# Two float32r parts instead of three bf16 parts for the first expert layer's up products

## The reference, cut to what matters

```
h      = xn @ Wm + bm                       # 128 features = 8 heads of 16
t      = h.reshape(tokens * 8, 16)
w      = softmax(t @ expert_emb)            # 16 experts, the best two kept
hmid   = gelu(einsum('td,edi->tei', t, W1) + b1)   # the up products: 16 -> 64, all 16 experts
eo     = einsum('tei,eio->teo', hmid, W2) + b2     # the down products: 64 -> 16
out    = (weights of the best two) * eo, summed over experts, then @ Wo + bo
```

## Time and profile before

| | us |
|---|---|
| median of 3 runs (lowest, highest) | 1351.73 (1351.6, 1356.91) |
| span of the profiled execution, first to last instruction | 1317.6 |
| difference of the two, outside the span | 34.1 |
| PE, DVE, ACT, POOL busy in the span | 1206.5, 1050.7, 891.2, 482.3 |
| first up product, last up product | 53.2, 532.4 |
| first instruction of the second layer | 548.4 |

### The profile page before, as it was taken

The page is one execution under the profiler, slowest core; times in us unless marked ns, Lnnn a source line. Parts: engine busy times, 40 slices in busy tenths (PEclk is TensorE's granted clock), DMA queues, the critical chain, the costliest instruction groups (busy, mean ns, idle before and its releaser), DMA issues. The chain is left out here.

```text
span 1317.6 us, 28397 instructions
## 1 busy us (share of the span) xinstructions
PE 1206.5 (92%) x11172; PEld 593.3 (45%) x11172; DVE 1050.7 (80%) x1954; ACT 891.2 (68%) x1246; POOL 482.3 (37%) x446
## 2 busy tenths in 40 slices
PE   6888998899988989798899999999899999999988
PEld 3333332333433323365555555555456544555434
DVE  4589789869898779769977799778787798787863
ACT  3668997898877888643266676666666666666666
POOL 3542554345514872320155511555025550000170
PEclk8889998999999999989999999999999999999999
DMA  6333322233332343248364544556335453233020
GB/s 224 116 117 125 106 94 101 92 109 101 100 103 94 111 132 106 93 118 233 106 183 136 174 122 117 151 139 157 87 101 160 133 142 89 72 82 105 19 64 28
DMA packets 129876, 152.88 MB, mean 116 GB/s; under 512 B 16048, under 2 KB 90800, under 8 KB 129616
## 3 DMA queue, kind: packets, MB, share of 16 engines
q1 hardware_dynamic: 111104, 127.50, 32.9%
q0 software_dynamic: 8192, 16.79, 4.3%
q10 hardware_dynamic: 10448, 6.77, 1.7%
HBM read 109.20 MB, written 41.81 MB: 115 GB/s over the span
## 5 line engine op out<-in xcount | busy, mean ns | idle before, releaser
L2887 ACT ACTIVATE ax_prob<-second_pair 128x1024 f32<-128x1024 f32 (+1 forms) x320 | 292.9, 939 | 146.4 <-PE second_pair L2840 94.4
L528 ACT ACTIVATE m_act_h<-first_pair,const 128x1024 f32<-128x1024 f32 x256 | 270.1, 1114 | 57.7 <-PE first_pair L482 44.1
L2764 DVE TENSOR_REDUCE am_top<-second_pair 128x2 f32<-128x1024 f32 (+1 forms) x192 | 222.9, 1175 | 38.6 <-PE second_pair L2718 25.5
L3019 POOL DMA_INDIRECT slot_tokens<-xn,mr_slots x128 | 124.0, 969 | 273.7 <-PE second_bank L1877 86.2
L3049 POOL DMA_INDIRECT m_back<-slot_results,mr_slots x128 | 122.2, 955 | 243.2 <-PE second_pair L2718 167.7
L482 PE MATMUL first_pair<-m_terms,w1s 96*128 96x512 bf16 x512 | 145.9, 391 | 19.6 <-ACT m_act_h L528 19.4
L2826 PE MATMUL ax_sums<-ax_prob,al_vs 128*32 128x512 f32 (+3 forms) x1536 | 161.2, 500 | 1.8 <-ACT ax_prob L2887 1.6
L494 PE MATMUL first_pair<-m_act_h,const 128*32 128x512 f32 x1024 | 130.4, 610 | 7.0 <-DVE m_prod L543 4.9
L582 POOL TENSOR_TENSOR m_both<-m_prod,m_both 128x512 f32<-128x512 f32 x64 | 86.7, 1371 | 123.8 <-DVE m_both L543 123.8
L2863 PE MATMUL second_pair<-al_qs,al_ks 51*128 51x512 bf16 (+3 forms) x768 | 115.9, 329 | 12.8 <-DVE am_top L2764 4.3
L2718 PE MATMUL second_pair<-al_ks,al_qs 48*128 48x512 bf16 (+3 forms) x768 | 116.2, 327 | 7.6 <-DVE am_top L2764 3.7
(11 more groups left out here) (396 smaller groups left out, 2515.1 us busy)
## 6 DMA issues: line engine op xcount, KB each, us to landing
m_wt<-in_experts SPq DMA_DIRECT2D x96, 384.0 KB
m_share<-shares SPq DMA_DIRECT2D x128, 256.0 KB
m_rows<-slot_tokens SPq DMA_DIRECT2D x60, 128.0 KB
slot_results<-m_y SPq DMA_DIRECT2D x60, 128.0 KB
stack<-mp_part SPq DMA_DIRECT2D x48, 128.0 KB
m_terms<-stack SPq DMA_DIRECT2D x64, 96.0 KB, 3.7
qstack<-ap_qpart SPq DMA_DIRECT2D x48, 128.0 KB
al_qs<-qstack SPq DMA_DIRECT2D x32, 192.0 KB, 3.9
```

Of the source, the lines that this page charges most:

```text
L528: A.activation(self.act_h[:, slot, :, :], banks.bank("up", n, ep)[:, :, :], ACT.Gelu, bias=self.w("b1", 4 * half + ep, 4 * half + ep + 1)) ...
L2764: V.tensor_reduce(into[:, 2 * a:2 * a + 2, at], tile[:, :, 0:n], AX, ALU.max, negate=True).then_inc(*banks.empties("max", i, m))
L2887: A.activation(dst, src, ACT.Exp, scale=SCALE).then_inc(*banks.empties("sum", i, u))
L3019: G.indirect_dma_start(self.tokens[g], bass.IndirectOffsetOnAxis(ap=self.route.slots[g][second][:, i:i + 1], axis=0), self.entry.zn(GC * g ...
```

## The change

The operands of the up products become float32r (a 4-byte format of TensorE with a shortened mantissa), in two parts each: high, and what the high part leaves. Four terms (all pairs of the two parts) are stacked, 4 x 16 = 64 rows, so that two heads stand in 128 rows. A step's two products go to the upper and the lower 64 rows of the array, with the weights repeated there.

- Moe0Prepare: the middle part and its two operations go. The high part and the rest (written over h) are float32r. Making the next tile's h waits until this tile's blocks are sent. Four DMAs of 256 KB a tile instead of six of 128 KB.
- m_terms: two slots, each with both heads of a pair (32 DMAs of 256 KB), instead of six slots with one head (64 of 96 KB).
- Moe0Weights: two parts in 128 rows, one cast, one subtraction, one addition; two ScalarE scalings instead of three.
- The planner is told of an up step of 0.23 (0.44 before) of class "rows", which before stood in the full class, of one preparation step fewer on ScalarE and on GpSimd, and of the DMAs. Wished times stay. The second layer keeps its six bf16 terms under new names (Q_TERMS, Q_PARTS, K_PARTS). A table PREP that nothing read is deleted.

```diff
-TERMS = 6
-ACT_PARTS = (0, 0, 1, 1, 0, 2)
-WEIGHT_PARTS = (0, 1, 0, 1, 2, 0)
+TERMS = 4
+ACT_PARTS = (0, 1, 0, 1)
+WEIGHT_PARTS = (0, 0, 1, 1)
+Q_TERMS, Q_PARTS, K_PARTS = 6, (0, 0, 1, 1, 0, 2), (0, 1, 0, 1, 2, 0)
...
-            a.wait_ge(self.lo_made, i)
+            a.wait_ge(self.parts_sent, i * 16 * TERMS)
             A.activation(self.h[:, :], banks.bank("h", i), ACT.Identity, bias=self.w("bm")).then_inc(*banks.empties("h", i))
...
-            A.activation(self.parts[0][:, :], self.h[:, :], ACT.Copy).then_inc(self.hi_made, 1)
-            yield FIRST["mid", i]
-            a.wait_ge(self.rest_made, i + 1)
-            A.activation(self.parts[1][:, :], self.h[:, :], ACT.Copy).then_inc(self.mid_made, 1)
+            A.activation(self.hi[:, :].bitcast(F32R), self.h[:, :], ACT.Copy).then_inc(self.hi_made, 1)
...
-            G.tensor_tensor(self.h[:, :], self.h[:, :], self.parts[0][:, :], ALU.subtract).then_inc(self.rest_made, 1)
-            yield FIRST["lo", i]
-            g.wait_ge(self.mid_made, i + 1)
-            G.tensor_tensor(self.parts[2][:, :], self.h[:, :], self.parts[1][:, :], ALU.subtract).then_inc(self.lo_made, 1)
+            G.tensor_tensor(self.h[:, :].bitcast(F32R), self.h[:, :], self.hi[:, :], ALU.subtract).then_inc(self.lo_made, 1)
...
-    TERM_SLOTS, SHARE_SLOTS, ACT_SLOTS = 6, 3, 8
+    TERM_SLOTS, SHARE_SLOTS, ACT_SLOTS = 2, 3, 8
...
+                q = n // 2
+                e.wait_ge(self.terms_landed[q % slots], 16 * (q // slots + 1))
                 for j in range(2):
-                    q = 8 * (n // 8) + 2 * hp + j
-                    e.wait_ge(self.terms_landed[q % slots], 16 * (q // slots + 1))
-                    p = E.matmul(banks.bank("up", n, ep)[:, j, :], self.w1s[:, (4 * half + ep) * P:(4 * half + ep + 1) * P], self.terms[:, q % slots, :], start=True, stop=True)
+                    rows = slice(TERMS * FD * j, TERMS * FD * (j + 1))
+                    p = E.matmul(banks.bank("up", n, ep)[:, j, :], self.w1s[rows, (4 * half + ep) * P:(4 * half + ep + 1) * P].bitcast(F32R),
+                                 self.terms[rows, q % slots, :].bitcast(F32R), start=True, stop=True)
                 p.then_inc(banks.filled, 1)
...
-TILES = {"sum": "rows", "max": "rows", "weigh": "columns", "maxturn": "columns", "k": "columns", "logits2": "columns",
+TILES = {"sum": "rows", "max": "rows", "up": "rows", "weigh": "columns", "maxturn": "columns", "k": "columns", "logits2": "columns",
...
-            pe("up", ("up", n, ep), at, 0.44, *[("terms", 8 * i + 2 * hp + j) for j in range(2)], *([("gelu", *divmod(u - 3, 4))] if u >= 3 else []), lag=0.2, fills=2)
+            pe("up", ("up", n, ep), at, 0.23, ("terms", n // 2), *([("gelu", *divmod(u - 3, 4))] if u >= 3 else []), lag=0.2, fills=2)
```

More of the change, by code:

```diff
@@ L8 @@
 BF16 = mybir.dt.bfloat16
+F32R = mybir.dt.float32r
 U32 = mybir.dt.uint32
@@ L227, in __init__ @@
         sb = lambda name, width=TILE, dt=F32: k.sb(f"mp_{name}", [P, width], dt, ctx=c)
-        self.h, self.parts = sb("h"), [sb(f"part{m}", dt=BF16) for m in range(3)]
+        self.h, self.hi = sb("h"), sb("hi")
+        self.parts = self.hi, self.h
         self.logits, self.one, self.rest, self.eq = sb("logits"), sb("one"), sb("rest"), sb("eq", dt=BF16)
@@ L390, in __init__ @@
         self.k, self.w, self.w1s = k, w, w1s
[L391 to L394, removed]
+        self.w1f = k.sb("mw_w1f", [P, FE * FI], ctx=c)
+        self.parts = [k.sb(f"mw_part{n}", [P, FE * FI], ctx=c) for n in range(2)]
         self.got, self.split, self.chosen = k.sem("mw_got"), k.sem("mw_split"), k.sem("mw_chosen")
@@ L420, in scalar @@
         a.wait_ge(const0, 16)
-        a.wait_ge(self.split, (2, 4, 4)[n])
-        A.activation(part[:, :], part[:, :], ACT.Copy, scale=self.w(f"rows{n}")[0:self.rows]).then_inc(self.chosen, 1)
+        a.wait_ge(self.split, 2)
+        A.activation(part[:, :], part[:, :], ACT.Copy, scale=self.w(f"rows{n}")).then_inc(self.chosen, 1)
 TILE_OF = [0, 1, 4, 5, 2, 3, 6, 7]
@@ L452, in sync_terms @@
         S, s, slots = self.k.nc.sync, self.k.sp, self.TERM_SLOTS
-        for q in range(NT * FH):
+        for q in range(NT * FH // 2):
+            i, hp = divmod(q, FH // 2)
             yield FIRST["terms", q]
             if q >= slots:
-                s.wait_ge(*self.banks.full("up", 2 * ((q - slots) // 2) + 1, 3))
-            s.wait_ge(self.prep.parts_sent, 16 * TERMS * (q // FH + 1))
-            S.dma_start(self.terms[:, q % slots, :], self.stack[ORDER[q // FH], q % FH, :, :]).then_inc(self.terms_landed[q % slots], 16)
+                s.wait_ge(*self.banks.full("up", 2 * (q - slots) + 1, 3))
+            s.wait_ge(self.prep.parts_sent, 16 * TERMS * (i + 1))
+            S.dma_start(self.terms[:, q % slots, :], self.stack[ORDER[i], 2 * hp:2 * hp + 2, :, :].rearrange("h r c -> (h r) c")).then_inc(self.terms_landed[q % slots], 16)
     def sync_shares(self):
@@ L1989, in sync @@
             s.wait_ge(self.split_q, 3 * c + 3)
-            for m in range(TERMS):
-                S.dma_start(self.qstack[b, :, m * AD:(m + 1) * AD, cols], self.q_parts[ACT_PARTS[m]][half]).then_inc(self.sent[c], 16)
+            for m in range(Q_TERMS):
+                S.dma_start(self.qstack[b, :, m * AD:(m + 1) * AD, cols], self.q_parts[Q_PARTS[m]][half]).then_inc(self.sent[c], 16)
             s.wait_ge(self.split_k, 3 * c + 3)
-            for m in range(TERMS):
-                S.dma_start(self.kstack[b, m * AD:(m + 1) * AD, cols], self.k_parts[WEIGHT_PARTS[m]][32 * half:32 * half + AD, :]).then_inc(self.sent[c], 16)
+            for m in range(Q_TERMS):
+                S.dma_start(self.kstack[b, m * AD:(m + 1) * AD, cols], self.k_parts[K_PARTS[m]][32 * half:32 * half + AD, :]).then_inc(self.sent[c], 16)
             s.wait_ge(*banks.done("v", c))
@@ L2239, in plan_units @@
         i, at = n // 8, unit_at(n)
-        for j in range(2):
-            q = 2 * n + j
-            if half == 0:
-                term = 8 * i + 2 * hp + j
-                sp("terms", ("terms", term), at - 10.0, 0.47, ("send", i), *([("up", 2 * ((term - Moe0.TERM_SLOTS) // 2) + 1, 3)] if term >= Moe0.TERM_SLOTS else []), lag=3.4)
+        if half == 0:
+            term = n // 2
+            sp("terms", ("terms", term), at - 10.0, 0.5, ("send", i), *([("up", 2 * (term - Moe0.TERM_SLOTS) + 1, 3)] if term >= Moe0.TERM_SLOTS else []), lag=3.4)
         for ep in range(4):
             u = 4 * n + ep
-            pe("up", ("up", n, ep), at, 0.44, *[("terms", 8 * i + 2 * hp + j) for j in range(2)], *([("gelu", *divmod(u - 3, 4))] if u >= 3 else []), lag=0.2, fills=2)
+            pe("up", ("up", n, ep), at, 0.23, ("terms", n // 2), *([("gelu", *divmod(u - 3, 4))] if u >= 3 else []), lag=0.2, fills=2)
             act("gelu", ("gelu", n, ep), at, 1.03, ("up", n, ep), *([("down", (u - Moe0.ACT_SLOTS) // 4, 1)] if u >= Moe0.ACT_SLOTS else []), lag=0.18, frees=("up", n, ep), table="g")
@@ L3458, in arrays @@
               ("b1", g0["b1"].reshape(EP, P).T), ("b2", g0["b2"].reshape(2, P).T), ("bo", col(g0["bo"]))]
-    for n in range(3):
-        parts.append((f"rows{n}", col(np.repeat(np.array([p == n for p in WEIGHT_PARTS], f32), FD))))
+    for n in range(2):
+        parts.append((f"rows{n}", col(np.tile(np.repeat(np.array([p == n for p in WEIGHT_PARTS], f32), FD), 2))))
     w2 = np.zeros((EP, 2, FI, 2, FD), f32)
```

51 lines of the change are left out of this document (18 added, 33 removed).

## The result

The changed kernel takes **1387.46 us** (median of 4 runs, 1382.28 to 1395.73) beside 1352.31 (4 runs, 1351.6 to 1356.91) of the kernel before: ratio 1.0259, 95% interval 1.0221 to 1.0297. It is 35 us slower; 15 faster was forecast.

The account below looks back on a forecast made before the run. No engine was taken to bound the whole first layer; PE led about 180 of 480 us. PE relief -12 and head -3 made -15: span 1302.6, time 1337 us, range 1318 to 1358.

Parts of the forecast that it names:

- The step's price: First layer's up products: a step streams 0.22 us instead of 0.44, so 256 steps save 56 us of PE.
- rival 1: Up products: float32r streams at 0.43 us a pass, so nothing is saved and the time is 1365, slower; chance 0.12.
- The borders: Up runs beside other PE work: tiling changes (98 of 0.09 us) and exposed weight loads (0.11 each) give back 30 us.
- The head: Start up to the first up product: shorter preparation and four stores instead of six bring it near 49.5, worth -3 us.
- Costed at nothing: Items priced at zero: weights, HBM traffic, SyncE's queue, making h only after the sends, and layer 2.
- Making h only after the sends: First-layer preparation: the next h's wait for the sends costs nothing, as a tile's units last 60 us and its sends a few.
- The -12 us: First-layer gain from PE relief: 9.7 in PE-led stretches, 1.6 in the level one, 1 in the ScalarE one.
- What 26 us of PE are worth: Section turning the net PE saving (56 less 30, 5.4% of 480 us) into 12 us of first-layer time.
- Rival 3: PE's relief lowers its clock in the first layer, costing 11 us of PE: 1345 to 1350; chance 0.20 together with rival 2.
- Rival 2: First layer: the list scheduler gives the PE gain away, the -12 vanish: 1350, the same; chance 0.20 together with rival 3.
- The weight loads: Up products: 0.11 us exposed at tiling borders; if float32r loads were fast, net PE saving about 40 instead of 26.
- The 34.1 us: Whole kernel: gap between the profiled span, 1317.6 us, and the runs' median, 1351.7, carried over unchanged.

Follow-up runs that it names:

- e12: e9 with each store cut to the first 256 columns (128 KB), which the loads read twice: ratio 0.9946 to the kernel before.
- e13: e5 (half-height product pairs issued twice) with stores cut to 128 KB, read twice by the loads: ratio 1.0027 to the kernel before.
- e14: e4 (half-height product pairs issued once) with stores cut to 128 KB, read twice by the loads: ratio 0.9938 to the kernel before.
- e17: The kernel of e14 (128 KB stores) run again beside e16 on one chip: 1346.40 us, ratio 0.9939 to the kernel before.
- e16: The kernel of e4 (256 KB stores) run again beside e17 on one chip: 1369.46 us, ratio 1.0114 to the kernel before.
- e1: The changed kernel with its first-layer steps in the order of the kernel before: ratio 1.0322 to the kernel before.
- e7: The changed kernel, full result, with other scheduler wishes found by search (first layer planned at 488 us instead of 508): ratio 1.0089 to the kernel before.
- e0: The kernel before, run again with no edit: ratio 1.0012, profiled execution 1352.23 us.
- e5: e4 with each pair of up products issued twice: ratio 1.015 to the kernel before.
- e4: e1 with only the high part stored (four times) and the low part not sent, so h need not wait: ratio 1.0123 to the kernel before.
- e3: e1 (changed kernel in the old order) with each pair of up products issued twice: ratio 1.0441 to the kernel before.
- e2: The changed kernel in its own order with each pair of up products issued twice: ratio 1.0407 to the kernel before.
- e8: e6 with each pair of up products issued twice: ratio 1.0177 to the kernel before.
- e11: The kernel before with scheduler wishes found by the same kind of search (planned at 505): ratio 1.0003 to the kernel before.
- e9: e4 with each up product over all 128 rows, two in series, no change of array tiling: ratio 1.0105 to the kernel before.
- e6: The kernel before with its bf16 up products on 32 rows, two heads at once, two thirds of the terms left out: ratio 1.0032.

## Why the prediction was wrong

The 35 us as a path from the kernel before to the changed one, each step the difference of two ratios times 1352. All but the last keep the old order:

| step | from | us |
|---|---|---|
| prepare with two parts, 4-byte products, one load per pair of heads, four stores of 128 KB | before to e12 | -7 |
| borders between array tilings | e12 to e13 | +11 |
| up products' stream time halved | e13 to e14 | -12 |
| stores of 256 KB | e14/e17 to e16 | +24 |
| h made only after the stores have landed | e16 to e1 | +28 |
| the new order and its plan | e1 to the changed kernel | -9 |

That the sum is +35 follows from the way it is built and proves nothing. The runs are from different chips, each beside its own before, so single terms are good to about 5 us. The first and the fourth term belong together: their meeting point stores a third less than the kernel before, so against the kernel before the stores carry less than 24. A version with that kernel's 768 KB a tile wasn't run. The path goes through the old order; the last term is that of the first plan tried, and with e7's it would be -32. The runs of the first four terms leave out the low part's product values, not an instruction of PE; the fifth step adds the low part and the wait for it.

*What held.* The step's price: two heads run together, a pair streams in 0.23, and rival 1 (0.43) is out. The borders: 0.50 for a first step, and 1.12 for the next product of full height. The head: first up product at 50.02, 49.5 forecast, if not by the way forecast (the first load goes out at 47.32 instead of the implied 44.7, but its data is there sooner). Layer 2: 790.1 us in e0, 795.3 after, 795.9 in e17; it was not touched.

*The step that failed* stands under "Costed at nothing": "Making h only after the sends: a tile's units last 480 / 8 = 60 us, and its sends a few". It compared averages. The h copy is not placed anywhere in those 60 us but at one place in ScalarE's queue, behind the previous tile's sends by as little as the old order allowed: 40.0 us of waits in five tiles (e1), with gelu behind them, 28 us of time. The new plan moves h back, and the direct wait is gone. In 50 to 560 us of the changed kernel:

```profile
ACT m_act_h L508 <- PE first_pair L461: 76.7, 57, 6.5
...
DVE m_both L523 <- DMA m_share<-shares: 7.7, 3, 3.5
...
ACT mp_h L255 <- DMA stack<-mp_h: 0.9, 1, 0.9
```

but only 9 of the 28 us come back. In the same stretch of e1 gelu waits much less for up products:

```profile
ACT m_act_h L508 <- PE first_pair L461: 44.6, 38, 3.3
```

So in the new order the loss stands mainly as gelu waiting for PE. It is not that h or its parts come too late: the last tile's h is made at 338.85 (318.35 in e0), but its stores go out at 369.67 (371.75 in e0), over 150 us before its first up product near 528 (496 in e0), and PE waits for loaded terms once, 2.7 us, at the start.

```profile
338.85 0.67 ACT L255 ACTIVATE mp_h<-first_pair,const 128x512 f32<-128x512 f32 x1
...
369.67 0.60 SPq L363 DMA_DIRECT2D stack<-mp_hi  x1
```

From the first up product to the last the plan of the changed kernel takes 476 us and the trace 533; for the kernel before it is 471 and 487 (e0), for e7 459 and 499. What makes the changed kernel fall 57 us behind its plan, with the clock at 0.90 in 60 to 540 instead of 0.96, stays open; no run takes the wait or the long stores out of the new order.

*The second* is in the head: "four stores instead of six, 3.86 x 4/6". It counted issues and left out the bytes. The stores went from 128 KB each to 256 KB, 768 KB in all to 1024, and take 8.7 us instead of 6.8 from the first issue to the first load. In the first tile little depends on it. With the seven others it is 24 us in the old order (e14 or e17 to e16), where the copy of the high part waits for the stores of the tile before: 18.3 us in e16, 3.5 in e17.

*The -12 us* under "What 26 us of PE are worth" were mis-sized. The saving of 56 us and the borders' cost came one by one as -12 and +11, hence nearly nothing, where 26 us of PE net were taken at 0.46. Over all pairs 56 us of products are worth 4 (e5 to e4), 12 (e13 to e14), 16 (e3 to e1) and 20 us (e2 to the changed kernel), a rate of 0.07 to 0.36. That the stretches led by PE are too short for more is argued, not measured. Rival 3 takes its part: between the two kernels of each pair the clock falls by 0.012 to 0.018. It named a cost of 11 us; at 9 us for each 0.01 the changed kernel's 0.02 go with 17 to 18 of the 35 us. That is no further term in the table, and which part of it is cause and which comes from longer waits can't be told from these runs. The Trainium skill ("TensorE: Matmul & The Clock Gate", Part 1: The HAM clock gate) says that the clock follows how busy the engine has been; e4's 0.951 against e5's 0.9685 agrees, e8's 0.949 does not.

*Rival 2*, that the scheduler gives the gain away, is right for the plan: it is 508.4 us before and 508.3 after, although PE's planned work fell from 442.8 to 389.1 us. The freed time became idle time in the plan. It doesn't explain the loss alone, as the old order is no better for the new products (e1). But its weight is large: e7, another plan for the same kernel, loses 12 us instead of 35, while the same search finds nothing for the kernel before (e11).

*The weight loads.* The prediction left open whether float32r loads would be fast ones. Each takes 183 ns (median of 512) in the changed kernel, the bf16 ones of e0 98: the slow, 4-byte case, with which the sum was made. So the other reading of the fast weight load in the Trainium skill ("TensorE: Matmul & The Clock Gate", Weight-path perf modes), 40 instead of 26 us, falls. That the load is exposed only across a border was wrong: e9 shows the 0.10 without one. It weighs little, since e12 has it too and is faster than the kernel before.

*The 34.1 us* carried over beside the span were a wrong premise: 1.7 us lie outside, and the rest is that the profiled execution was faster than the median. By chance this doesn't alter the forecast difference, but every share read from it (five stretches at clock 1.00) came from a better case than the median one. A small slip beside it: the engine behind PE in 420 to 480 is 4.6 us below it, not 4.7.

## What to carry over

Where an edit turns a scratch buffer into the source of a transfer, so that its next writer must wait until the transfer has landed, find the next writer of that buffer in its engine's queue and price the wait there, by the landing of the stores in bytes and not by their number; a cover given as an average over the tile is no cover. Here, work taken from an engine that leads in few stretches arrived at 7 to 36% of its size. And where a scheduler orders the work, search its wishes anew for both kernels before judging the change: this was worth 23 us to one and nothing to the other. The runs point to a version that wasn't run: each part stored once (two stores of 256 KB a tile, as many bytes as e17's) and read twice by the loads, with a second buffer for the low part. From e17 an estimate for it is 0.6% at most, in the old order, and memory for that buffer must be found first.

## What the runs showed of the hardware

- A float32r product streams 512 columns in 0.22 to 0.24 us, like bf16, at 64 rows (in pairs) and at 128. Its weight load lasts 183 ns (changed kernel, 64x128, median of 512) against 98 for bf16 (e0, 96x128).
- Two chips differ by 2.3% for the same kernel (medians of 1322 and 1352 us), with the granted clock at 0.974 and 0.966; in the profiled executions of e12 and e0 the second layer alone, the same instructions, takes 769.0 and 790.1 us.
- From execution to execution the kernel before takes 8.4 to 10.6 us more for each 0.01 of granted clock, by chip; the changed kernel about 16, from four executions.
- A kernel that issues its up products twice instead of once has a granted clock higher by 0.012 to 0.018 (four pairs with float32r); with bf16 on 32 rows (e6, e8) it is higher by 0.004 only.
